# Cross-attention and table-decoded feed-forward layer: keys of all batches first, two batches per product

## The reference

```python
h = layernorm(x)
q = rope(h @ wq)            # 32 heads of 128
k, v = rope(ctx @ wk), ctx @ wv   # 8 heads of 128, each shared by 4 query heads
p = softmax(q @ k.T / sqrt(128) + mask)
x = x + (p @ v) @ wo
# feed-forward: a 1024 x 1024 matrix, each weight decoded from 4 bit planes
# through a table of 16 values per output row
w = lut4[o, bits of qweight[0:4]]
x = x + layernorm(x) @ w.T + bias
```

## Time and profile before

| what | us |
|---|---|
| median of three runs | 2343.17 |
| the profiled execution's own time | 2341.57 |
| its span | 2339.8 |
| TensorE busy | 2326.8 |
| VectorE busy | 1693.0 |
| ScalarE busy | 1115.5 |
| GpSimd busy | 572.5 |

### The profile page before, as it was taken

The page is one execution under the profiler, slowest core; times in us unless marked ns, Lnnn a source line. Parts: engine busy times, 40 slices in busy tenths (PEclk is TensorE's granted clock), DMA queues, the critical chain, the costliest instruction groups (busy, mean ns, idle before and its releaser), DMA issues.

```text
span 2339.8 us, 35189 instructions
## 1 busy us (share of the span) xinstructions
PE 2326.8 (99%) x11902; PEld 1989.4 (85%) x11902; DVE 1693.0 (72%) x3811; ACT 1115.5 (48%) x2472; POOL 572.5 (24%) x675
## 2 busy tenths in 40 slices
PE   9999999999999999999999999999999999999999
PEld 8999998888888888888888888888888888888887
DVE  7888777677776777777776767677767776777763
ACT  5555544546464646455544444444444444444110
POOL 1000001322323233232333233323332332331320
PEclk9999999999999999999999999999999999999999
DMA  7466559444444343434457634333433333334442
GB/s 259 158 197 216 193 172 304 156 127 119 116 135 118 109 130 108 129 107 127 116 162 231 220 94 125 93 109 98 126 92 108 107 106 108 91 112 161 155 135 81
DMA packets 330098, 328.26 MB, mean 140 GB/s; under 512 B 32448, under 2 KB 266176, under 8 KB 329920
## 3 DMA queue, kind: packets, MB, share of 16 engines
q1 hardware_dynamic: 294496, 309.88, 42.7%
q10 hardware_dynamic: 35424, 16.14, 2.7%
HBM read 181.73 MB, written 71.30 MB: 108 GB/s over the span
## 4 chain that ended last, share of the span: by engine, by line
PE 96%; DVE 2%; DMA 1%; ACT 1%; issue 0%; POOL 0%; SPq 0%; ACTq 0%; DVEq 0%
PE bank L926 29%; PE bank L840 29%; PE bank L794 8%; PE bank L966 7%; PE bank L856 7%; PE bank L897 7%; PE bank L771 7%; DMA small_split<-probs 0%; PE bank L732 0%; DMA ln_row<-in_L_xattn_wk 0%; POOL probs L1947 0%; DVE residual L1811 0%; PE bank L752 0%; PE bank L871 0%; DMA k_scratch<-small_split 0%
## 5 line engine op out<-in xcount | busy, mean ns | idle before, releaser
L840 PE MATMUL bank<-acts_split,weights_split 128*128 128x512 f32 (+1 forms) x3192 | 742.9, 382 | 0.0
L926 PE MATMUL bank<-weights_split,small_split 128*128 128x512 f32 x3072 | 741.2, 390 | 1.6 <-DVE small_split L1795 1.6
L926 PEld LDWEIGHTS bank<-weights_split,small_split 128*128 128x128 f32 x3072 | 574.3, 188 | 121.4 <-DVE small_split L1795 2.8
L840 PEld LDWEIGHTS bank<-acts_split,weights_split 128*128 128x128 f32 x3192 | 576.5, 188 | 109.4
L1947 POOL TENSOR_SCALAR probs<-probs,row_numbers 128x256 f32<-128x256 f32 x512 | 361.6, 719 | 1188.7 <-DVE row_numbers L1781 1188.7
L1259 ACT ACTIVATE probs<-bank,row_numbers 128x256 f32<-128x256 f32 x512 | 238.1, 472 | 122.5 <-DVE row_numbers L1776 121.7
L1785 DVE STREAM_TRANSPOSE probs<-probs 128x512 f32<-128x512 f32 x250 | 177.7, 711 | 146.9 <-POOL probs L1947 146.9
L1939 POOL TENSOR_TENSOR rope_x<-rope_x,sin_t 128x512 f32<-128x512 f32 (+1 forms) x133 | 167.0, 1256 | 402.2 <-ACT rope_x L1232 402.1
L1770 DVE CUSTOM_DVE_ANT_0 bank<-bank,mask_tile 128x256 f32<-128x256 f32 x512 | 207.2, 446 | 65.5 <-PE bank L856 65.2
L856 PEld LDWEIGHTS bank<-small_split 128*128 128x128 f32 x1536 | 217.9, 190 | 22.3 <-DVE small_split L1750 2.5
L1790 DVE TENSOR_TENSOR small_split<-small_split 128x512 fp32r<-128x512 f32 x250 | 179.2, 717 | 76.2 <-ACT small_split L1272 76.0
(11 more groups left out here) (124 smaller groups left out, 2167.5 us busy)
## 6 DMA issues: line engine op xcount, KB each, us to landing
small_split<-probs SPq DMA_DIRECT2D x754, 64.0 KB, 2.2
raw<-in_L_xattn_wq SPq DMA_DIRECT2D x61, 512.0 KB, 3.7
raw<-in_L_xattn_wo SPq DMA_DIRECT2D x60, 512.0 KB, 3.7
k_scratch<-small_split SPq DMA_DIRECT2D x64, 256.0 KB, 2.3
v_scratch<-small_split SPq DMA_DIRECT2D x32, 512.0 KB, 2.9
x_scratch<-raw SPq DMA_DIRECT2D x64, 256.0 KB, 2.8
acts_split<-x_scratch SPq DMA_DIRECT2D x32, 512.0 KB, 5.3
mask_tile<-in_mask_BxSxS_ff SPq DMA_DIRECT2D x64, 256.0 KB, 2.9
```

The source lines that it names most:

```text
L840: last = pe.matmul(query_bank(j)[:, 0:wide], wq_s[:, h, c, a, :], xT[:, c, m, b * S:b * S + wide], start=c == 0 and i == 0, stop=c == C - ...
L926: last = pe.matmul(out_ps[part][:, :], o_s[:, a, u % 2 * S + t * P:u % 2 * S + (t + 1) * P], wo_s[:, h, m, n * BANK:(n + 1) * BANK], start ...
```

## The change

- The stage has 64 steps (`A_STEPS`), one product of 24 matmuls of 512 columns in each. Steps 0 to 31 are keys: a pair of batches by a head. Steps 32 to 63 are values, in four segments of eight, one pair of batches in each, in the order `V_PAIRS`.
- The split context of a pair of batches is 8 times 512 numbers in both parts, half of `W` or of `X` (`ctx_slots`). It no longer fits beside all the weights. So the context of pair 3 stays from its keys to its values, and that of pairs 0, 1 and 2 is loaded and split a second time for their values. `wv` is loaded and split when halves of `X` and `W` come free (steps 24 to 31).
- GpSimd multiplies by all key sines. It also makes the low parts of the 8 pieces of `wv` and of the 12 context pieces in the value steps.
- Decoding is placed over steps 5 to 57 by a planner. It has a cost for each kind of operation, in units of 10 ns, and takes 515 a step less what else VectorE has there. The result tile alternates (`roles`).
- Each key step has ScalarE's rounding (`keys_high`) of its own key ahead of the next key's swap. One decoding operation stands between `rope_cos` and `rope_add`.
- Nine rows of `x` are begun six steps apart, from step 4 (`ROW_BASE`), and are turned four steps after.
- Values, keys and decoded weights have their own staging and their own counts of stores.
- In attention, one query job is moved from unit 2 to unit 1, a few transfers are placed otherwise, and the residual rows of the second half are loaded 8 units later.
- There are 30 warm-up transposes in place of 24.

```diff
-    A_ROPES = NB * HKV
+    A_ROPES = NB // 2 * HKV
+    V_GROUPS = NB * TS * NN
+    A_STEPS = A_ROPES + V_GROUPS
+    V_PAIRS = (3, 0, 1, 2)
+    CTX_STEP = (3, 4, 5, 6, 10, 11, 12, 13, 18, 19, 20, 21,
+                33, 34, 35, 36, 41, 42, 43, 44, 49, 50, 51, 52)
+    PIECE_STEP = (0, 1, 2, 3, 4, 24, 25, 26, 27, 28, 29, 30, 31)
+    SPLIT_AT = {step: HEAD_PIECES + n for n, step in enumerate(PIECE_STEP)}
+    QUERY_AT = {A_STEPS - REP + h: h for h in range(REP)}
+    ROW_BASE = tuple(4 + 6 * e for e in range(9))
-    WARM = 24
+    WARM = 30
+    for step in range(5, A_STEPS):
+        spent = min(spent, 150) + 515 - (215 if step < A_ROPES else 70)
+        spent -= 125 * ((step in CTX_AT and step < A_ROPES) + (step in SPLIT_AT and step < 24) + (step in QUERY_AT))
+        spent -= sum(150 for base in ROW_BASE if step in (base + 4, base + 5))
+        spent -= sum(150 for end in ENDED.values() if step == end + 2)
+        DECODE[step] = []
+        while n < NB * TREE and spent > 0:
+            tile, op = n // TREE, n % TREE
+            DECODE[step].append((tile, op))
+            spent -= 170 if op == 0 else 20 if op == 1 else 135 if op in (4, 7, 8, 11, 14, 15, 16) else 85
+            n += 1
...
+            if op == 0:
+                break
+    TURN_AT = {end + 2: tile for tile, end in ENDED.items()}
...
-                    WORK[u - AHEAD] = [(j, range(C))]
-                    WORK[u - AHEAD + 1] = [(j + 1, range(C))]
+                    WORK[u - AHEAD] = [(j, range(C)), (j + 1, range(C))]
...
             # SP
+            load_context(0)
+            load_split(0)
+            for q in range(1, CTX_HEAD):
+                load_context(q)
+            for k in range(1, HKV):
+                load_split(k)
...
+            for tick in range(2, A_STEPS + 1):
+                if 0 <= tick - 2 < A_ROPES:
+                    store_keys(tick - 2)
+                if tick in CTX_AT:
+                    load_context(CTX_AT[tick])
+                if tick in ROW_STEP:
...
+                    load_row(ROW_STEP[tick])
...
             # TensorE
+            def keys(j):
+
+                pair, g = j // HKV, j % HKV
+                if g < HKV and pair == 0:
+                    pe.wait_ge(w_lo, g + 1)
+                pe.wait_ge(rope_cosd, j + 1)
+                for c in range(C):
+                    if g == 0 and c % 4 == 0:
+                        pe.wait_ge(ctx_lo, 4 * pair + c // 2 + 2)
+                    for i, (a, m) in enumerate(PASSES):
+                        done = pe.matmul(k_ps[j % 2][:, :], wk_s[:, g, c, a, :], ctx_slots[pair][:, c, m, :],
+                                         start=c == 0 and i == 0, stop=c == C - 1 and i == 2)
+                done.then_inc(rope_mm, 1)
...
+            for step in range(A_STEPS):
+                if step < A_ROPES:
+                    keys(step)
+                else:
+                    values(step - A_ROPES)
+                if step - 4 in ROW_STEP:
+                    turn_row(ROW_STEP[step - 4])
+                if step in TURN_AT:
+                    turn_weights(TURN_AT[step])
...
             # ScalarE
+            for step in range(A_STEPS):
+                if step < A_ROPES:
+                    rope_swap(step, k_ps[step % 2], 1.0, step % 2, 2)
+                else:
+                    values_high(step - A_ROPES)
+                if step in SPLIT_AT:
+                    piece_hi(SPLIT_AT[step])
+                if step in CTX_AT:
+                    context_high(CTX_AT[step])
+                if step in TURN_AT:
+                    for i in range(2):
+                        weights_high(TURN_AT[step], i)
+                if step - 4 in ROW_STEP:
+                    x_high(ROW_STEP[step - 4], 0, x_ps[0])
+                if step < A_ROPES:
+                    keys_high(step)
+                if step - 2 in ROW_STEP:
+                    row_root(ROW_STEP[step - 2])
+                if step - 3 in ROW_STEP:
+                    row_norm(ROW_STEP[step - 3])
+                if step in ROW_STEP:
+                    row_mean(ROW_STEP[step])
+                    row_center(ROW_STEP[step])
+                if step - 1 in ROW_STEP:
+                    row_square_in_psum(ROW_STEP[step - 1])
+                if step - 5 in ROW_STEP:
+                    x_high(ROW_STEP[step - 5], 1, x_ps[1])
...
+                for tile in range(NB):
+                    if step == BEGUN[tile]:
+                        full_bit0(tile)
...
             # VectorE
+            for step in range(A_STEPS):
+                if step < A_ROPES:
+                    rope_cos(step)
+                ops = DECODE.get(step, ())
+                if step < A_ROPES:
+                    for tile, op in ops[:1]:
+                        decode(tile, op)
+                    ops = ops[1:]
+                    rope_add(step, step % 2)
+                else:
+                    values_low(step - A_ROPES)
+                if step in SPLIT_AT and SPLIT_AT[step] < HKV:
+                    piece_lo(SPLIT_AT[step])
+                if step in CTX_AT and step < A_ROPES:
+                    context_low(CTX_AT[step])
...
+                for tile, op in ops:
+                    decode(tile, op)
...
+                if step < A_ROPES:
+                    rope_low(step)
+                if step in QUERY_AT:
+                    query_lo(QUERY_AT[step])
...
             # GpSimd
+            for step in range(A_STEPS):
+                if step < A_ROPES:
+                    turned = fold(ropes[step % 2][0], (0, 1))
+                    pool.wait_ge(rope_in, 2 + step + 1)
+                    pool.tensor_tensor(turned, turned, table(sin_t, (0, 1)), ALU.mult).then_inc(rope_sind, 1)
+                if step in SPLIT_AT and SPLIT_AT[step] >= HKV:
+                    k = SPLIT_AT[step]
+                    pool.wait_ge(w_hi, k + 1)
+                    pool.tensor_tensor(a_piece(k)[:, :, LO, :], a_source(k), a_piece(k)[:, :, HI, :].bitcast(F32),
+                                       ALU.subtract).then_inc(w_lo, 1)
+                if step in CTX_AT and step >= A_ROPES:
+                    q = CTX_AT[step]
+                    pool.wait_ge(ctx_hi, q + 1)
+                    pool.tensor_tensor(ctx_piece(q)[:, :, LO, :], ctx_stage[ctx_place(q)],
+                                       ctx_piece(q)[:, :, HI, :].bitcast(F32), ALU.subtract).then_inc(ctx_lo, 1)
```

803 lines of the change are left out of this document (274 added, 529 removed).

## The result

| | kernel before | kernel after |
|---|---|---|
| median us (runs) | 2344.48 (4) | 2378.32 (4) |
| all runs us | 2341.26 to 2346.1 | 2376.16 to 2381.49 |
| profiled span us | 2339.8 | 2374.9 |
| query products start at us | 384.40 | 418.10 |
| from there to the end us | 1955.40 | 1956.80 |

The changed kernel is slower: ratio 1.0149, 95% interval 1.0137 to 1.0161, which is 33.8 us, or 35.1 us between the two profiled spans. Of these 35.1 us, 33.7 lie in the first stage and 1.4 behind it. The forecast was 2360.

A forecast was written before the change was run, and what follows sets the result against it. TensorE, 99% busy, was taken as the bound. Start 10.9 + work 363.6 + waits 27.6 = 402.1 against 384.4: +17.7, less 1 in attention = +16.7; 2343.2 + 16.7 = 2359.9, said as 2360 us, range 2338 to 2371.

The forecast's parts named there:

- TensorE's own work: First stage: 184.3 us of key products removed, 175.1 added, gain 9.2; 363.6 us of work in steps of 5.47.
- The head: Start of the first stage: first key product at 10.9 us, between 10 and 13, where it was 6.84.
- The waits at the row transposes: TensorE waits for row tiles 0 to 4 behind ScalarE's chain in key steps, 27.6 us together.
- the upper reading: Key steps: decoding operations and GpSimd block each other like the 1024-wide subtraction; waits 27.6 us, against 18.7 by the lower.
- Rival A: Key steps: only two-input arithmetic blocks between VectorE and GpSimd; +7.8 us, 2351, chance 0.15.
- rivals B: Key steps: VectorE and GpSimd pass each other or share the port; waits 5.4 us, time 2338, chance 0.14.
- C: First stage: all waits hidden, 9.9 + 1 us gained, time 2332, chance 0.14.
- rival D: VectorE's queue, not ScalarE's, sets the pace in steps 24 to 31; includes a clock fall; 2371 us, chance 0.07.
- The value steps: From step 32 on: row tiles 5 to 8 in time, GpSimd's context pieces 0 to 4 us, taken as 0.
- Attention: The moved query job fills a 2.3 us wait at unit 2's scores; gain 0 to 2.3 us, taken as 1.

The follow-up runs named there:

- run 9: The changed kernel with attention's turned rows and residual rows loaded at the units of the kernel before; 2379.14 us, ratio 1.0150 to the kernel before.
- runs 3: The changed kernel with unread identity transposes put in front of the waits for row tiles 0 to 4; 2378.11 us, ratio 1.0141 to the kernel before.
- run 2: The changed kernel with the low parts of the value weights made by VectorE instead of GpSimd; 2363.51 us, ratio 1.0083 to the kernel before.
- run 10: The changed kernel with ScalarE's row work before key roundings, value weights' low parts on VectorE, attention's query-job order and loads as before; 2343.11 us.

## Why the prediction was wrong in size and right in direction

- TensorE's own work: right. Steps of 5.48 us where nothing waits (144 products in 32.91), as costed. The sum had no term for the short gaps, 2.4 us.
- The head: right, 11.02 for 10.9 (10.5 to 11.7 in the runs with the new stage).
- The waits at the row transposes: right in place and cause, and in the total of 27.6 partly by luck. Tiles 0 to 2 were costed at 3.8, 2.2 and 3.3 and came at 3.77, 3.28 and 2.79. Tile 3 was costed at 6.1 and came at 6.60. It holds 1.5 us that the sum hadn't (at 175.48 ScalarE stands 0.48 for the spread bits and expands bit 0 for 1.06). Tile 4 was costed at 12.2 and took 8.51, or 10.2 at full clock (10.15 in run 9). The cosines, costed at nothing, took 1.76. So errors of both signs make up a total that is right within 1 us. The choice of the upper reading, that a decoding operation holds GpSimd off and is held off, was right. Rival A (7.8 us) is refuted by the leaf of 1.22 and the addition of 2.88, rivals B and C by the waits themselves.
- **The step that failed** is the term for the clock, which isn't in the sum at all: rival D spoke of a fall after waits of 6 and 12 us, "its price mostly hidden as the other engines catch up meanwhile". The fall came, and not only there: behind waits of 3.3 us on, and behind the 1.76 at the cosines. It cost some 11 us, seen in the lines that ran slow. Of these 1.7 were hidden (runs 3 and 9), so some 9.3 were missing from the sum; with the short gaps it is 11.7. The reason, which is read from the order of the steps and not tested by itself, is in the chain: it is late only in the four steps in front of a row tile. In the two steps in between, and just behind a tile, TensorE is the bound, and that is where it runs slow, so little is there to hide it. The Trainium skill (TensorE: Matmul & The Clock Gate, "Part 1") gives two levels, 1.2 GHz for an idle array and 2.4 GHz for a busy one. This trace agrees: 8 transposes at 1.97 and 1.04 to 1.09, about two to one, the first behind 6.60 and 8.51 us of idle time.
- The value steps, taken as 0, cost 3.3 us: two row tiles (0.80, 0.91) and one low part (1.63).
- Attention, taken as 1 us gained, came out at 1.4 lost between the two profiles, and about level at the medians. The gain is there (scores 1.4 us sooner from unit 5 on), and in the profile 2.8 are lost later, mostly by waits that the prediction had no step for (2.4 at L901).
- Together 9.3 + 2.4 + 3.3 + 2.4, with 0.1 at the start, and 0.8 for row waits that would have been longer still at full clock (28.4 for 27.6), are 18.3 of the 18.4 us by which the span went over the forecast's (35.1 for 16.7). The clock is half of it.

## What to carry to other kernels

When a change puts idle time into a matrix engine that had none, cost the slower clock behind each wait as time of its own, unless the profile names what else is late at that place: here some 11 us beside waits of 30, and 1.7 of the 11 were hidden. Where GpSimd and VectorE share a chain, count a decoding operation, or an arithmetic one with two SBUF inputs, as held nearly until the other engine's ends, and look at which of two independent operations reaches its turn first: 16.8 us went with eight subtractions moved to the busier engine (and some decoding moved later). Before reading a few microseconds from a profile, see where its execution lies among the others of the same kernel. In an ordered queue, put work with an early due time (the row tile) in front of an instruction that waits on a long chain: that alone was worth 23.6 us.

## What the runs showed of the hardware that was not expected

- A leaf, which has one SBUF tensor and a column per partition as inputs, is held off by GpSimd as the subtraction is: 1.22 for 0.81 (at 196.04). The cosine product beside it, with one operand in PSUM, isn't (0.69 at 195.44). A predicated copy takes up to 3.41 for 1.34. The Trainium skill (SBUF — State Buffer, "SBUF: two separate sides") has the lock held for the full instruction, and the trace agrees: the addition of 0.69 takes 2.88 behind a piece of 2.84.
- The clock fell also behind shorter waits: transposes of 1.97 stand behind 2.46, 2.80, 3.27 and 3.77 us in run 2, while in the changed kernel those behind 2.79 and 3.77 take 1.09. Behind the 3.77 the fall comes later there (144 products in 34.52), behind the 2.79 not at all (32.91). The length of the wait in front alone doesn't decide it. The plainest pair is the first units of attention, with the same wait and the same 36 products behind it. The timeline of TensorE in run 10:

```profile
406.23 0.94 PE L861 MATMUL bank<-small_split 128*128 128x256 f32 x6 [2.28 <-ACT probs L1194]
...
408.02 7.14 PE L845 MATMUL bank<-acts_split,weights_split 128*128 128x256 f32 x36
```

and in the kernel before:

```profile
407.50 0.94 PE L856 MATMUL bank<-small_split 128*128 128x256 f32 x6 [2.28 <-ACT probs L1259]
...
409.05 5.86 PE L840 MATMUL bank<-acts_split,weights_split 128*128 128x256 f32 x36
```

  The granted clock of that stretch is 0.81 in run 10 (406 to 415) and 1.00 in the kernel before (407 to 418).
